# Scores of the first two head groups during the projection, x normalised on ScalarE, and a last tile in halves

## The chip, the cores and the metric

The kernel runs on one core of a Trainium2 chip. Its engines are TensorE (PE, matmul; loading weights is listed as PEld), VectorE (DVE), ScalarE (ACT), GpSimd (POOL), and SyncE (SP), which here issues every DMA. The metric is the device time of one execution in microseconds (us), lower is better. The kernel before took 815.09 us, the median of 3 runs (814.35 to 815.36).

## The reference

One block of cross attention and a feed-forward with ternary weights, each with a residual. All tensors are float32; batch 4, 512 rows each of x (512 wide) and of the context (256 wide), 32 heads of 16.

```python
q = rope((layernorm(x) @ Wq)), k = rope(ctx @ Wk), v = ctx @ Wv      # (4, 512, 32, 16) each
w = softmax(einsum('bqhd,bkhd->bhqk', q, k) / 4)
x = x + einsum('bhqk,bkhd->bqhd', w, v) @ Wout + bout
def bitlinear(x, w):
    xn = layer_norm(x)
    return absmax_quant(xn) @ ternarize_weights(w).T                 # 8-bit rows, weights in -g, 0, +g
h = gelu(bitlinear(layernorm(x), w_fc))                              # 512 -> 2048
x = x + bitlinear(h, w_proj)                                         # 2048 -> 512
```

## The kernel before

The program is written engine by engine. Each engine has a fixed list of instructions in the order of its block function, and semaphores join the lists. Nothing is scheduled by a planner: the order of the code is the order of the work.

**Projection.** The 2048 rows are 16 tiles of 128 rows. A loop `for s in range(3, TILES + 3)` runs on every engine with the tiles shifted against each other. A stage of TensorE turns the context of tile s-2 (`turn_ctx`, L256) and its normalised x (`turn_x`, L264), turns the rotated k of tile s-4 (`turn_rotated`, L304), multiplies tile s-3 by Wk and Wv (`project_kv`), turns the rotated q of s-4 and multiplies by Wq (`project_q`). Products are split: each operand has a rounded high part and a low part, and `product` (L279) runs high by high, high by low and low by high. Rotation (RoPE) is three products on VectorE (`rope_products`, L394 to L396) and a sum on GpSimd (`sum_products`, L486). The turned result is cut into three bfloat16 parts: cast on ScalarE (L459), subtraction on VectorE (`take_first`, L404), cast on ScalarE (L462), subtraction on GpSimd (`last_part`, L490). The layer norm of x takes statistics on VectorE (L375, L378), the root on GpSimd (`spread`, L477, L480) and the normalisation on VectorE (`normalise`, L384). SP loads inputs and pieces of the FFN weights, whose absolute values ScalarE sums, and after each second tile stores the parts to DRAM (`store_parts`). From there `load_stacks` brings them back, rearranged, as stacks of 96 rows for a group of 4 heads of one batch; it has 7 DMAs a group. There are 32 groups and 4 stack slots.

**Attention.** A step s does three things on TensorE (`tensor_step`): scores of group s with queries on the partitions (`scores`, L643, 16 matmuls in 8 pairs, two slots of two PSUM banks), of which VectorE takes row maxima (`row_maxima`, L713); scores of group s-2 turned round, with the maxima already subtracted by two more rows in the stack (`scores_turned`, L669), of which ScalarE takes exponentials (L733); and their product with v (`weigh_v`, L682). Between these, GpSimd splits the maxima (`split_maxima`), TensorE turns them, ScalarE saves them, and a small DMA (`load_max`, L575) puts them into the stack. GpSimd also makes a ternary weight block each step (`ternarise`, L762 to L767) and stages v. Scores of group 0 stand after the last q product, between the last turns; step 1 has scores of group 1 only. The ternary weights need the sum of all absolute values, so a totals matmul and a few small operations (`add_totals`, `weigh_ffn`) lie there too.

**Rows.** For 16 tiles again: output projection (`mix`, L901), quantisation, `expand` (L915), GELU, statistics of h (`statistics`, L982, L987), centring (`centre_h`, L1045), the largest value (L995) and clipping (L1004, L1010) in `clip_h`, the second float16 part (`second_h`, L1016), transposing DMAs of both parts (`turn_h`, L883), `contract` (L927, 32 matmuls a tile), and `finish` (L1023). For the last tile nothing stands beside this chain but the contraction of tile 14.

## Time and profile before

| | us |
|---|---|
| median of 3 runs | 815.09 |
| the profiled execution | 815.23 |
| its span (first to last instruction) | 813.3 |
| TensorE busy | 782.3 |
| VectorE busy | 679.5 |
| ScalarE busy | 452.3 |
| GpSimd busy | 332.6 |
| mean granted clock of TensorE | 0.979 of 2.4 GHz |

The profile describes one execution. Times of its rows are microseconds from the start of the span. "Idle before" is how long the engine stood still before an instruction, and the arrow names what ended the wait. A granted clock of 1.00 is 2.4 GHz, 0.50 is 1.2 GHz. The instructions of a line are pipelined, so the listed durations of matmuls overlap; what one costs the engine is read from the distance of starts or from the chain.

### The profile page before, as it was taken

Reading aid. Unit: us, or ns where it says so; the run is one execution under the profiler, and the core shown is the slowest. Engines: PE = TensorE matmul, PEld = TensorE weight load, DVE = VectorE, ACT = ScalarE, POOL = GpSimd, SP = SyncE. Lnnn points to the kernel's source line nnn. Section 1 sums busy time; section 2 is a strip of 40 time slices with the busy share of each in tenths; the row PEclk is TensorE's granted clock in tenths of the full one; section 3 lists DMA queues with packets and bytes.
Section 4 is the critical chain, followed back from the end, with each engine's and each line's share of the span. In section 5 each row is a group of like instructions: output and inputs, shape, how many; then the busy total and the mean of one; then the engine's idle time right before and its main releaser. Section 6 shows DMA issues by size and latency. Waiting matters only on the chain.

```text
span 813.3 us, 11712 instructions
## 1 busy us (share of the span) xinstructions
PE 782.3 (96%) x3844; PEld 333.6 (41%) x3844; DVE 679.5 (84%) x940; ACT 452.3 (56%) x828; POOL 332.6 (41%) x428
## 2 busy tenths in 40 slices
PE   3999997999999999999999999899999999999996
PEld 3788884122222222222322232244444444444442
DVE  6888887888888888888888888269999998988983
ACT  5567664277777777777777777734223432233330
POOL 2687776724543554455445544323212211111000
PEclk9999998599999999999999999999999999999999
DMA  7588887545465554667656653325556546553463
GB/s 260 156 221 261 236 227 183 122 110 127 125 170 138 153 145 133 154 142 164 163 155 166 172 167 80 84 64 122 109 123 151 111 90 117 109 125 79 78 130 90
DMA packets 173677, 116.17 MB, mean 143 GB/s; under 512 B 114562, under 2 KB 145330, under 8 KB 173618
## 3 DMA queue, kind: packets, MB, share of 16 engines
q1 hardware_dynamic: 173618, 115.44, 57.0%
q8 instruction: 31, 0.51, 0.3%
q14 instruction: 28, 0.23, 0.1%
HBM read 64.50 MB, written 25.43 MB: 111 GB/s over the span
## 4 chain that ended last, share of the span: by engine, by line
PE 86%; DVE 7%; DMA 2%; ACT 2%; issue 2%; POOL 2%; SPq 0%; DVEq 0%; POOLq 0%; ACTq 0%
PE banks L682 15%; PE banks L669 15%; PE banks L643 13%; PE banks L915 11%; PE banks L279 11%; PE banks L927 10%; PE banks L901 7%; PE banks L304 2%; DVE h_scales L995 1%; DMA stack_words<-max_rows 1%; DVE maxima L713 1%; DVE h_stats L982 1%; ACT probs_words L733 1%; PE banks L264 1%; ACT probs_words L1045 1%
## 5 line engine op out<-in xcount | busy, mean ns | idle before, releaser
L713 DVE TENSOR_REDUCE maxima<-banks 128x2 f32<-128x1024 f32 x256 | 302.0, 1216 | 52.1 <-PE banks L643 52.0
L733 ACT ACTIVATE probs_words<-banks 128x512 f32<-128x512 f32 x512 | 276.0, 597 | 101.3 <-PE banks L669 99.4
L669 PE MATMUL banks<-stack_words 98*128 98x512 bf16 x512 | 175.6, 386 | 2.7 <-ACT probs_words L733 1.8
L643 PE MATMUL banks<-stack_words 96*128 96x512 bf16 x512 | 160.2, 395 | 4.5 <-DVE maxima L713 3.9
L682 PE MATMUL banks<-probs_words,late_words 128*32 128x512 f32 x1024 | 137.2, 608 | 0.5
L927 PE MATMUL banks<-ternary_words,stack_words 128*128 128x512 f16 x512 | 114.6, 383 | 4.5 <-DMA stack_words<-stack_words 4.5
L915 PE MATMUL banks<-ternary_words,late_words 128*128 128x512 f16 x512 | 113.1, 379 | 0.0
L1045 ACT ACTIVATE probs_words<-probs_words,h_moments 128x2048 f32<-128x2048 f32 x16 | 32.0, 2002 | 135.8 <-DVE h_moments L987 135.8
L669 PEld LDWEIGHTS banks<-stack_words 98*128 98x128 bf16 x512 | 39.5, 97 | 144.2 <-ACT probs_words L733 84.3
L747 POOL TENSOR_SCALAR neg_max<-maxima 128x16 f32<-128x16 f32 x32 | 8.3, 258 | 175.0 <-DVE maxima L713 175.0
L927 PEld LDWEIGHTS banks<-ternary_words,stack_words 128*128 128x128 f16 x512 | 50.5, 99 | 70.0 <-issue 13.5
L643 PEld LDWEIGHTS banks<-stack_words 96*128 96x128 bf16 x512 | 49.7, 99 | 69.2 <-DVE maxima L713 13.4
L915 PEld LDWEIGHTS banks<-ternary_words,late_words 128*128 128x128 f16 x512 | 50.1, 98 | 61.4 <-issue 1.7
L1068 POOL TENSOR_SCALAR h_powers<-h_moments 128x1 f32<-128x1 f32 x16 | 3.6, 224 | 155.0 <-DVE h_moments L987 155.0
L1039 ACT ACTIVATE probs_words<-banks,row_scale 128x512 f32<-128x512 f32 x64 | 42.5, 683 | 29.1 <-PE banks L915 29.0
L901 PE MATMUL banks<-v_words,attn_words 128*128 128x512 f32 x128 | 57.6, 593 | 0.0
L762 POOL TENSOR_SCALAR late_words<-late_words,limits 128x512 f16<-128x512 f32 x32 | 50.2, 1568 | 0.0
L764 POOL TENSOR_SCALAR late_words<-late_words,limits 128x512 f16<-128x512 f32 x32 | 50.1, 1565 | 0.0
L490 POOL TENSOR_TENSOR ternary_words<-attn_words,ternary_words 128x512 bf16<-128x512 f32 x32 | 37.3, 1167 | 23.0 <-ACT ternary_words L462 23.0
L682 PEld LDWEIGHTS banks<-probs_words,late_words 128*32 128x32 f32 x1024 | 20.2, 108 | 54.6 <-ACT probs_words L733 39.8
L486 POOL TENSOR_TENSOR attn_words<-attn_words 128x512 f32<-128x512 f32 x32 | 41.3, 1291 | 2.0 <-DVE attn_words L396 0.9
L995 DVE TENSOR_REDUCE h_scales<-probs_words 128x1 f32<-128x2048 f32 x16 | 36.4, 2272 | 4.3 <-ACT probs_words L1045 4.3
(129 smaller groups left out, 932.1 us busy)
## 6 DMA issues: line engine op xcount, KB each, us to landing
o_rows<-late_words SPq DMA_DIRECT2D x32, 256.0 KB, 2.8
k_parts<-ternary_words SPq DMA_DIRECT2D x48, 128.0 KB, 3.2
q_parts<-ternary_words SPq DMA_DIRECT2D x48, 128.0 KB, 2.5
stack_words<-q_parts SPq DMA_DIRECT2D x32, 192.0 KB, 3.0
stack_words<-k_parts SPq DMA_DIRECT2D x96, 64.0 KB, 2.7
stack_words<-k_parts SPq DMA_DIRECT2D x32, 192.0 KB, 2.8
attn_words<-in_x_dram SPq DMA_DIRECT2D x16, 256.0 KB, 4.2
probs_words<-in_L_ffn_w_fc_dram SPq DMA_DIRECT2D x16, 256.0 KB, 3.3
```

What stands on the lines that cost most here:

```text
L279: mm = self.nc.tensor.matmul(out, lhs[a][:, slot, k * P:(k + 1) * P], rhs[b][:, k, :], start=(a + b + k == 0), stop=(a == 1 and k == count ...
L643: mm = self.nc.tensor.matmul(self.score_slot[j % 2][:, i], self.mem.q_stack[0:STACK, slot, head, c * P:(c + 1) * P], self.mem.k_stack[0:ST ...
L669: self.nc.tensor.matmul(self.mem.banks[:, self.ST_BANK[k]], self.mem.k_stack[0:STACK + 2, slot, head, c * P:(c + 1) * P], self.mem.q_stack ...
L682: mm = self.nc.tensor.matmul(self.pv_bank[32 * j:32 * j + 32], self.v_ones[:, g % 2, c, j, :], self.probs[:, c, j, :], start=(c == 0), sto ...
L713: dve.tensor_reduce(self.maxima[:, g % 2, 2 * j:2 * j + 2], self.score_slot[j % 2], AX.X, ALU.max).then_inc(self.scores_read, 1)
L733: act.activation(self.probs[:, c, head, :], self.mem.banks[:, self.ST_BANK[k]], ACT.Exp, scale=1 / math.sqrt(HEAD)).then_inc(self.exp_done, 1)
L762: pool.tensor_scalar(self.below[:], self.raw[:, w], limits[:, 1, w:w + 1], None, ALU.is_lt).then_inc(self.cut, 1)
L764: pool.tensor_scalar(self.ternary[:, w], self.raw[:, w], limits[:, 0, w:w + 1], None, ALU.is_gt).then_inc(self.cut, 1)
L901: mm = self.nc.tensor.matmul(self.y_bank[n % 2], att.attnT[:, n // CHUNKS * KX + k, c * P:(c + 1) * P], self.wout_sb[:, k, :], start=(k == ...
L915: mm = self.nc.tensor.matmul(self.fc_bank[o], self.uT[:, n % U_SLOTS, part * KX + k], self.fcT[:, k, o], start=(k + part == 0), stop=(k == ...
L927: mm = self.nc.tensor.matmul(self.proj_bank[r], self.hT[:, r, part, k], self.projT[:, k // 2, k % 2], start=(k + part == 0), stop=(part == ...
L995: dve.tensor_reduce(scale(0), now, AX.X, ALU.max, apply_absolute_value=True).then_inc(self.h_step, 1)
```

## The change

- Scores of groups 0 and 1 are taken as 32 single matmuls (`early_scores`), each into PSUM bank 7, each read by a reduction over 512 values (`early_maxima`) before the next may write. In the stages s = 10 to 18 of the projection there are three a stage; five more stand among the last turns and after them. The stacks of the groups 0 to 3 are loaded in the stages 8, 10, 13 and 15. The maxima of group 0 are split, turned, saved and loaded at the end of the projection. The attention loops begin with step 2.
- `normalise` moves from VectorE to ScalarE, between the two casts of k (`first_two` becomes `first_part` and `second_part`); GpSimd gets a third small instruction in `spread` for its bias.
- At the start `project_kv` is cut in two, so that the k product stands ahead of turning x; GpSimd takes the high parts of Wq for k = 1 and 3.
- ScalarE no longer waits for the stored parts; SP does, before its attention loop. GpSimd splits the maxima of group 1 and stages v before the first ternarisation.
- The last tile is centred, reduced, clipped, split and turned in two halves of 1024 columns, and its statistics come ahead of `second_h` of tile 14.

```diff
+    def normalise(self, act, n):
+        r = n % 2
+        act.wait_ge(self.rstd_ready, n + 1)
+        need(act, self.x_turned, n - 1)
+        act.activation(self.xn[:, r], self.x_sb[:, n % INPUT_SLOTS], ACT.Identity, bias=self.rstd[:, r, 2:3],
+                       scale=self.rstd[:, r, 1:2]).then_inc(self.xn_ready, 1)
...
+    def weight_high_too(self, pool, loaded, high, raw, ready):
+        pool.wait_ge(loaded, DMA)
+        pool.tensor_copy(high, raw).then_inc(ready, 1)
...
                            ).then_inc(self.power_ready, 1)
         pool.wait_ge(self.power_ready, n + 1)
         pool.tensor_tensor(self.rstd[:, r, 1:2], self.rstd[:, r, 0:1], self.mem.half_power[:], ALU.pow
+                           ).then_inc(self.power_taken, 1)
+        pool.wait_ge(self.power_taken, n + 1)
+        pool.tensor_scalar(self.rstd[:, r, 2:3], self.moments[:, r, 0:1], self.rstd[:, r, 1:2], -1.0, ALU.mult, ALU.mult
                            ).then_inc(self.rstd_ready, 1)
...
+    def early_scores(self, pe, i):
+
+        g, head, c = i // (GH * CHUNKS), i // CHUNKS % GH, i % CHUNKS
+        if i % (GH * CHUNKS) == 0:
+            pe.wait_ge(self.stacks_loaded[g], STACK_LOADS)
+        need(pe, self.early_read, i)
+        self.nc.tensor.matmul(self.early_bank, self.mem.q_stack[0:STACK, g, head, c * P:(c + 1) * P],
+                              self.mem.k_stack[0:STACK, g, head, :], start=True, stop=True).then_inc(self.early_ready, 1)
+
+    def turn_first_max(self, pe):
+        pe.wait_ge(self.split_ready, 1)
+        self.nc.tensor.transpose(self.early_max_bank, self.max_parts[:, 0], self.mem.identb[:]).then_inc(self.max_turned, 1)
...
-        if g == 0 and k == self.ST_BANK.index(self.TURN_BANK):
-            pe.wait_ge(self.max_saved, 1)
-        elif k != self.after_turn:
+        if g == 0 and k < 3:
+            pe.wait_ge(self.prj.multiplied[1], TILES)
+            for side in range(2):
+                pe.wait_ge(self.prj.rest_done[side], TILES)
...
+    def early_maxima(self, dve, i):
+        g, at = i // (GH * CHUNKS), i % (GH * CHUNKS)
+        dve.wait_ge(self.early_ready, i + 1)
+        dve.tensor_reduce(self.maxima[:, g, at:at + 1], self.early_bank, AX.X, ALU.max).then_inc(self.early_read, 1)
...
-        pool.wait_ge(self.scores_read, (g + 1) * 2 * GH)
+        if g < self.EARLY:
+            pool.wait_ge(self.early_read, (g + 1) * GH * CHUNKS)
+        else:
+            pool.wait_ge(self.scores_read, (g + 1 - self.EARLY) * 2 * GH)
...
+    def turn_last(self, sp, part, half):
+        n, k = TILES - 1, FFN // P // 2
+        r, done = n % 2, self.h_first if part == 0 else self.parts_ready
+        sp.wait_ge(done, n + 1 + half)
+        if part + half == 0:
+            need(sp, self.proj_ready, n - 1)
+        sp.dma_start_transpose(self.hT[:, r, part, half * k:(half + 1) * k], self.h_parts[:, r, part, half * HALF:(half + 1) * HALF]
+                               ).then_inc(self.last_turned[part][half], DMA)
...
+        for half in range(2):
+            dve.wait_ge(self.h_centred, n + 1 + half)
+            dve.tensor_reduce(self.half_max[:, half:half + 1], halves[half], AX.X, ALU.max, apply_absolute_value=True
+                              ).then_inc(self.halves_read, 1)
+        dve.wait_ge(self.halves_read, 2)
...
+        for half in range(2):
+            dve.tensor_scalar(halves[half], halves[half], scale(2), Q_B, ALU.mult, ALU.min).then_inc(self.last_clipped, 1)
+            dve.wait_ge(self.last_clipped, 1 + half)
+            dve.tensor_scalar(self.h_parts[:, r, 0, half * HALF:(half + 1) * HALF], halves[half], -Q_B, None, ALU.max
+                              ).then_inc(self.h_first, 1)
...
+            part = self.h_parts[:, r, :, half * HALF:(half + 1) * HALF]
+            dve.wait_ge(self.h_first, n + 1 + half)
+            dve.scalar_tensor_tensor(part[:, 1], halves[half], -Q_B, part[:, 0], ALU.max, ALU.subtract
+                                     ).then_inc(self.parts_ready, 1)
...
-                if s in (14, 16):
-                    att.load_stacks(sp, s // 2 - 7)
-            att.load_stacks(sp, 2)
-            att.load_stacks(sp, 3)
+                if s in (8, 10, 13, 15):
+                    att.load_stacks(sp, (8, 10, 13, 15).index(s))
+                if s == TILES + 3:
+                    att.load_max(sp, 0)
+            for pair in range(2):
+                sp.wait_ge(prj.parts_stored[pair], PAIR_STORES * BATCH)
...
-                    prj.project_kv(pe, s - 3)
+                    prj.project_k(pe, s - 3)
+                if s == TILES + 2:
+                    att.turn_first_max(pe)
+                if s >= 10:
+                    att.early_scores(pe, 3 * (s - 10))
+                if 1 <= s - 3 < TILES:
+                    prj.project_v(pe, s - 3)
                 if within(s - 4, TILES):
                     prj.turn_rotated(pe, s - 4, 1)
+                if s >= 10:
+                    att.early_scores(pe, 3 * (s - 10) + 1)
                 if within(s - 3, TILES):
                     prj.project_q(pe, s - 3)
-            att.scores(pe, 0, 0)
+                if s >= 10:
+                    att.early_scores(pe, 3 * (s - 10) + 2)
             prj.turn_rotated(pe, TILES - 1, 0)
-            att.scores(pe, 0, 1)
+            att.early_scores(pe, 27)
             prj.turn_rotated(pe, TILES - 1, 1)
-            att.scores(pe, 0, 2)
...
+            for i in range(28, att.SINGLES):
+                att.early_scores(pe, i)
+            pe.wait_ge(att.early_read, att.SINGLES)
             prj.add_totals(pe)
-            for j in range(3, 2 * GH):
-                att.scores(pe, 0, j)
-
-            for s in range(1, GROUPS + 3):
+
+            for s in range(2, GROUPS + 3):
                 att.tensor_step(pe, s)
                 if s >= GROUPS:
...
+                if s > 10:
+                    att.early_maxima(dve, 3 * (s - 11) + 2)
...
-                if within(s - 1, TILES):
-                    prj.normalise(dve, s - 1)
+                if s >= 10:
+                    att.early_maxima(dve, 3 * (s - 10))
                 if s < TILES:
...
+            prj.rope_products(dve, TILES - 1, 1)
+            att.early_maxima(dve, 26)
+            prj.take_first(dve, TILES - 1, 0)
+            att.early_maxima(dve, 27)
             prj.sum_ffn(dve)
-            prj.rope_products(dve, TILES - 1, 1)
-            att.row_maxima(dve, 0, 0)
-            prj.take_first(dve, TILES - 1, 0)
-            att.row_maxima(dve, 0, 1)
+            att.early_maxima(dve, 28)
             prj.take_first(dve, TILES - 1, 1)
-            att.row_maxima(dve, 0, 2)
+            for i in range(29, att.SINGLES):
+                att.early_maxima(dve, i)
             prj.weigh_ffn(dve)
-            for j in range(3, 2 * GH):
...
+                if s == TILES:
+                    rows.clip_last(dve)
+                    rows.finish(dve, s - 3)
+                    rows.split_last(dve)
...
-                    prj.first_two(act, s - 4, 0)
+                    prj.first_part(act, s - 4, 0)
+                if within(s - 1, TILES):
+                    prj.normalise(act, s - 1)
+                if within(s - 4, TILES):
...
-            for pair in range(2):
-                act.wait_ge(prj.parts_stored[pair], PAIR_STORES * BATCH)
...
+            att.split_maxima(pool, 1)
+            pool.wait_ge(prj.projected[1], TILES)
             pool.memset(att.v_ones, 1.0).then_inc(att.pads_ready, 1)
             pool.wait_ge(att.pads_ready, 1)
+            pool.wait_ge(prj.v_saved, TILES)
+            att.stage_v(pool, 0)
             for s in range(GROUPS + 1):
-                if s >= 1:
```

The order on TensorE in one stage of the projection, from the last part of the k product on (wk, wv and wq are the weights, ident is the matrix that turns a tile, stack_words holds the stacks). Before:

```order
L279 MATMUL banks<-wk_high,ctxT_low 128x512 x2
L279 MATMUL banks<-wv_high,ctxT_high 128x512 x2
L279 MATMUL banks<-wv_low,ctxT_high 128x512 x2
L279 MATMUL banks<-wv_high,ctxT_low 128x512 x2
L304 MATMUL banks<-ident,attn_words 128x128 x4
L279 MATMUL banks<-wq_high,xT_high 128x512 x4
L279 MATMUL banks<-wq_low,xT_high 128x512 x4
L279 MATMUL banks<-wq_high,xT_low 128x512 x4
L256 MATMUL banks<-ident,attn_words 128x128 x2
```

and now:

```order
L282 MATMUL banks<-wk_high,ctxT_low 128x512 x2
L679 MATMUL banks<-stack_words 128x512
L282 MATMUL banks<-wv_high,ctxT_high 128x512 x2
L282 MATMUL banks<-wv_low,ctxT_high 128x512 x2
L282 MATMUL banks<-wv_high,ctxT_low 128x512 x2
L311 MATMUL banks<-ident,attn_words 128x128 x4
L679 MATMUL banks<-stack_words 128x512
L282 MATMUL banks<-wq_high,xT_high 128x512 x4
L282 MATMUL banks<-wq_low,xT_high 128x512 x4
L282 MATMUL banks<-wq_high,xT_low 128x512 x4
L679 MATMUL banks<-stack_words 128x512
L259 MATMUL banks<-ident,attn_words 128x128 x2
```

Three score matmuls (L679) have come in, one before the v product, one before the q product, and one after it.

The order on VectorE around the same place, with the RoPE products (the first three rows, PSUM banks in, attn_words out), then the low parts and the subtraction. Before:

```order
L394 TENSOR_TENSOR attn_words<-banks,ternary_words 128x512
L395 TENSOR_TENSOR attn_words<-banks,ternary_words 128x64x4
L396 TENSOR_TENSOR attn_words<-banks,ternary_words 128x64x4
L416 TENSOR_TENSOR ctxT_low<-banks,ctxT_high 128x256
L423 TENSOR_TENSOR xT_low<-banks,xT_high 128x512
L404 TENSOR_TENSOR attn_words<-banks,ternary_words 128x512
L384 TENSOR_SCALAR ternary_words<-attn_words,project_moments,rstd 128x512
L375 BN_STATS project_stats<-attn_words 128x6
L378 BN_AGGR project_moments<-project_stats 128x2
L394 TENSOR_TENSOR attn_words<-banks,ternary_words 128x512
L395 TENSOR_TENSOR attn_words<-banks,ternary_words 128x64x4
L396 TENSOR_TENSOR attn_words<-banks,ternary_words 128x64x4
```

and now:

```order
L395 TENSOR_TENSOR attn_words<-banks,ternary_words 128x512
L396 TENSOR_TENSOR attn_words<-banks,ternary_words 128x64x4
L397 TENSOR_TENSOR attn_words<-banks,ternary_words 128x64x4
L753 TENSOR_REDUCE maxima<-banks 128x1
L417 TENSOR_TENSOR ctxT_low<-banks,ctxT_high 128x256
L424 TENSOR_TENSOR xT_low<-banks,xT_high 128x512
L405 TENSOR_TENSOR attn_words<-banks,ternary_words 128x512
L753 TENSOR_REDUCE maxima<-banks 128x1
L382 BN_STATS project_stats<-attn_words 128x6
L386 BN_AGGR project_moments<-project_stats 128x2
L395 TENSOR_TENSOR attn_words<-banks,ternary_words 128x512
L396 TENSOR_TENSOR attn_words<-banks,ternary_words 128x64x4
```

The normalisation (L384) is gone from the stage, and three reductions (L753) have come, one of them ahead of the low parts of context and x.

The order on TensorE at the end of the projection, from the last third of the last q product on (L311 and L318 now are the turns and the totals). Before:

```order
L279 MATMUL banks<-wq_high,xT_low 128x512 x4
L643 MATMUL banks<-stack_words 128x512 x2
L304 MATMUL banks<-ident,attn_words 128x128 x4
L643 MATMUL banks<-stack_words 128x512 x2
L304 MATMUL banks<-ident,attn_words 128x128 x4
L643 MATMUL banks<-stack_words 128x512 x2
L311 MATMUL banks<-abs_sum,ones 128x2
L643 MATMUL banks<-stack_words 128x512 x18
L652 MATMUL banks<-identb,max_parts 32x128
L643 MATMUL banks<-stack_words 128x512 x8
L669 MATMUL banks<-stack_words 128x512
```

and now:

```order
L282 MATMUL banks<-wq_high,xT_low 128x512 x4
L679 MATMUL banks<-stack_words 128x512
L311 MATMUL banks<-ident,attn_words 128x128 x4
L679 MATMUL banks<-stack_words 128x512
L311 MATMUL banks<-ident,attn_words 128x128 x4
L679 MATMUL banks<-stack_words 128x512 x4
L318 MATMUL banks<-abs_sum,ones 128x2
L709 MATMUL banks<-stack_words 128x512
L668 MATMUL banks<-stack_words 128x512 x2
L709 MATMUL banks<-stack_words 128x512 x3
L668 MATMUL banks<-stack_words 128x512 x2
```

32 score matmuls (L643, those of groups 0 and 1) stood between the last q product and the first turned scores (L669). Now six single ones (L679) and the totals stand there, and then step 2 begins (L709, L668).

The order on VectorE for the last tile (h_scales are its scales, probs_words is h, stack_words its parts). Before:

```order
L1006 SCALAR_TENSOR_TENSOR out_scale<-h_scales,gamma 128x1
L1010 TENSOR_SCALAR stack_words<-probs_words 128x2048
L1016 SCALAR_TENSOR_TENSOR stack_words<-probs_words,stack_words 128x2048
L982 BN_STATS h_stats<-probs_words 128x6 x4
L987 BN_AGGR h_moments<-h_stats 128x2
L1023 SCALAR_TENSOR_TENSOR v_words<-banks,out_scale,late_words 128x512
L995 TENSOR_REDUCE h_scales<-probs_words 128x1
L997 RECIPROCAL h_scales<-h_scales 128x1
L999 TENSOR_SCALAR h_scales<-h_scales 128x1
L1001 SCALAR_TENSOR_TENSOR h_scales<-h_scales,h_powers 128x1
L1004 TENSOR_SCALAR probs_words<-probs_words,h_scales 128x2048
L1006 SCALAR_TENSOR_TENSOR out_scale<-h_scales,gamma 128x1
```

and now:

```order
L1047 BN_STATS h_stats<-probs_words 128x6 x4
L1052 BN_AGGR h_moments<-h_stats 128x2
L1081 SCALAR_TENSOR_TENSOR stack_words<-probs_words,stack_words 128x2048
L1095 TENSOR_REDUCE v_words<-probs_words 128x1 x2
L1098 TENSOR_TENSOR h_scales<-v_words 128x1
L1100 RECIPROCAL h_scales<-h_scales 128x1
L1102 TENSOR_SCALAR h_scales<-h_scales 128x1
L1106 TENSOR_SCALAR probs_words<-probs_words,h_scales 128x1024
L1108 TENSOR_SCALAR stack_words<-probs_words 128x1024
L1106 TENSOR_SCALAR probs_words<-probs_words,h_scales 128x1024
L1108 TENSOR_SCALAR stack_words<-probs_words 128x1024
L1133 SCALAR_TENSOR_TENSOR v_words<-banks,out_scale,late_words 128x512
```

The statistics of tile 15 have moved ahead of the second part of tile 14 (L1081), and the reduction and the clipping are done in halves.

## Rows read from the trace of the kernel before

**Rows 1.** Page part 1, busy time and share of the span by engine.

```profile
PE 782.3 (96%) x3844; PEld 333.6 (41%) x3844; DVE 679.5 (84%) x940; ACT 452.3 (56%) x828; POOL 332.6 (41%) x428
```

**Rows 2.** Windows: us, busy (xinstructions) by engine, granted clock, DMA share; one stage.

```profile
75.79:82.85 7.06, 7.06 (x39) 5.93 (x38) 6.06 (x13) 4.88 (x12) 5.63 (x6) 1.00 0.89 278
```

**Rows 3.** Timeline, TensorE, turning ctx: start, us, engine, line, what.

```profile
82.85 0.38 PE L256 MATMUL banks<-ident,attn_words 128*128 128x128 f32 x2
...
89.92 0.38 PE L256 MATMUL banks<-ident,attn_words 128*128 128x128 f32 x2
```

**Rows 4.** Windows of 10 us at the end of the projection.

```profile
130.00:140.00 10.00, 6.42 (x28) 3.15 (x27) 8.76 (x15) 3.17 (x6) 6.17 (x6) 0.80 0.69 176
...
150.00:160.00 10.00, 9.06 (x23) 2.27 (x26) 8.29 (x8) 4.10 (x7) 9.69 (x11) 0.50 0.33 81
```

**Rows 5.** Chain of waits in order of time, 126 to 172: start, us, what.

```profile
131.82 0.45 PE banks L643 x2
...
151.63 2.68 DMA stack_words<-max_rows
...
154.44 0.59 PE banks L669
...
169.34 0.22 PE banks L669
```

**Rows 6.** Page part 5, costliest groups: busy us, mean ns, idle before.

```profile
L713 DVE TENSOR_REDUCE maxima<-banks 128x2 f32<-128x1024 f32 x256 | 302.0, 1216 | 52.1 <-PE banks L643 52.0
```

**Rows 7.** Chain of waits in order of time, 760 to the end.

```profile
786.36 2.48 DVE h_stats L982 x4
...
796.61 4.47 DMA stack_words<-stack_words
...
801.21 8.77 PE banks L927 x32
```

**Rows 8.** Windows of 2 us in the last contraction.

```profile
802.00:804.00 2.00, 2.00 (x6) 0.76 (x5) 0.00 (x0) 0.00 (x0) 0.00 (x0) 0.50 1.09 329
```

**Rows 9.** Timeline, TensorE, contraction of tiles 13 and 14.

```profile
782.77 13.98 PE L927 MATMUL banks<-ternary_words,stack_words 128*128 128x512 f16 x64
```

**Rows 10.** Timeline of the start, GpSimd and TensorE.

```profile
8.10 2.16 POOL L480 TENSOR_TENSOR rstd<-rstd,half_power 128x1 f32<-128x1 f32 x1
...
19.66 0.90 PE L264 MATMUL banks<-ident,ternary_words 128*128 128x128 f32 x4 [2.53 <-DVE ternary_words L384]
...
25.61 2.51 POOL L486 TENSOR_TENSOR attn_words<-attn_words 128x512 f32<-128x512 f32 x2
...
26.93 0.66 PE L304 MATMUL banks<-ident,attn_words 128*128 128x128 f32 x4 [1.62 <-POOL attn_words L486]
```

**Rows 11.** Groups by line, 60 to 130: busy us, mean ns | idle before.

```profile
L490 POOL TENSOR_TENSOR ternary_words<-attn_words,ternary_words 128x512 bf16<-128x512 f32 x20 | 23.4, 1168 | 13.3 <-ACT ternary_words L462 13.3
L404 DVE TENSOR_TENSOR attn_words<-banks,ternary_words 128x512 f32<-128x512 f32 x20 | 13.7, 686 | 6.5 <-issue 6.5
...
L462 ACT CAST ternary_words<-attn_words 128x512 bf16<-128x512 f32 x20 | 12.4, 619 | 20.0 <-DVE attn_words L404 20.0
...
L480 POOL TENSOR_TENSOR rstd<-rstd,half_power 128x1 f32<-128x1 f32 x8 | 4.5, 567 | 0.7
L384 DVE TENSOR_SCALAR ternary_words<-attn_words,project_moments,rstd 128x512 f32<-128x512 f32 x8 | 4.3, 538 | 0.0
```

**Rows 12.** Timeline of SP: load of x, loads of one group's stacks.

```profile
60.33 0.45 SPq L205 DMA_DIRECT2D attn_words<-in_x_dram  x1
...
101.23 1.45 SPq L570 DMA_DIRECT2D stack_words<-q_parts  x3
102.73 1.81 SPq L570 DMA_DIRECT2D stack_words<-k_parts  x4
```

**Rows 13.** DMA issues from 740 on: count, median us to landing.

```profile
stack_words<-stack_words SPq DMA_TRANSPOSE x10, 4.4
late_words<-late_words SPq DMA_TRANSPOSE x2, 3.1
```

184 lines of the change are left out of this document (124 added, 60 removed).

## The prediction

> **What bounds the kernel now.** I read the busy shares first. The reader is to see there that TensorE is busy nearly all of the span [rows 1]. So time can be saved only where it waits, works at its lower clock, or does work that could go; VectorE (DVE), with the second-largest share, is the one to follow next.
>
> Next the tables by stretch. In the projection (16 tiles, about 26 to 132 us) one stage of 7.06 us holds 7.06 us of TensorE, 6.06 of VectorE, 4.88 of ScalarE and 5.63 of GpSimd [rows 2]. The same instruction of two neighbouring stages starts 7.07 us apart [rows 3]. TensorE sets the pace there, and VectorE has 1.0 us to spare in each stage.
>
> Between 130 and 155 us TensorE works little and falls from 2.4 to 1.2 GHz: granted clock 0.80 in 130 to 140, 0.50 in 150 to 160 [rows 4]. The chain of waits tells why [rows 5]: after the last projection at 131.82 come row maxima of groups 0 and 1, sixteen reductions on VectorE of 1.22 us each [rows 6], and the hand-over of the maxima (POOL, DMA). The first turned scores run at 154.44, and the second attention step begins at 169.34, so that the step before it takes 14.9 us.
>
> At the end the chain leaves TensorE again [rows 7]: statistics of the last tile from 786.36, centring, reduction and clipping, a transposing DMA from 796.61 that lands 4.47 us later, then 32 matmuls in 8.77 us instead of 6.9, because the clock was granted at 0.50 in 802 to 804 [rows 8]. The 64 matmuls of tiles 13 and 14 took 13.98 us [rows 9].
>
> The profiled execution took 815.23 us: 813.3 of span and 1.9 around it. That is 0.14 above the median of the three runs (815.09), so I may work from it.
>
> **Term 1, the start: -1.7 us (0 to -2.5).** Now the k product of tile 0 stands ahead of turning its x, ScalarE normalises, GpSimd makes two of four high parts of Wq, and ScalarE's list is shorter. Today x of tile 1 is turned at 19.66, and GpSimd's first two RoPE sums run at 25.61, so TensorE can turn rotated k only at 26.93 [rows 10]. Walking the new lists: ScalarE has normalised tile 1 at about 17.3 (v of tile 0 is out at 15.0, then a copy, a cast and the normalisation, some 0.6 each). VectorE ends the four low parts of Wq at 20.0 instead of 21.5, since it no longer normalises between them. The statistics of tile 3 follow at 21.8, GpSimd's reciprocal root (one small instruction longer, 0.3) ends at 23.8, and its first sum at 25.1 instead of 26.9. If the GpSimd copies come late, nothing is left.
>
> GpSimd's power of 0.57 us [rows 11] took 2.16 at 8.10 [rows 10], while VectorE subtracted two SBUF tensors. The Trainium skill ("SBUF — State Buffer", section on the two separate sides) says that VectorE with two SBUF inputs and GpSimd hold one port pair as an exclusive lock. The trace agrees (2.16 against 0.57). By that rule the two new copies on GpSimd and the subtractions for Wq would block each other; that is rival B.
>
> **Term 2, the projection: +5.8 us (+5.5 to +8).** 26 of the 32 early score matmuls now stand before the end of the last q product, three a stage in stages 10 to 18 but for the last of them. One costs TensorE what it costs now: a pair at 131.82 took 0.45 us at full clock [rows 5], 0.22 each. 26 x 0.22 = 5.7, and the transposed maxima of group 0 add 0.1. Nothing hides this, since TensorE has no gap there. A stage becomes 7.07 + 0.66 = 7.73 us.
>
> Is VectorE still under it? It loses the normalisation, 0.54 us [rows 11], and gains three reductions over 512 values. No row shows a single one from PSUM. Below, it is half the double one, 0.61; above, the whole 1.22 [rows 6]; I take 0.66, as half of it and a small fixed part, since the 512-wide subtractions from PSUM last 0.69 [rows 11]. So 6.06 - 0.54 + 3 x 0.66 = 7.50 us, 0.2 under TensorE. At 1.22 each it would be 9.2 and 9 stages would cost 13 us more; the neighbours of the same width speak against that. The other loop: turn rotated k, cast, subtract, cast, then on GpSimd the third part (1.17), the root (now about 1.2) and the sum (1.26, half of the two at 25.61) [rows 10, 11], until rotated k is turned again. With the reduction that now stands ahead of the subtraction I get 7.5 us for it, also 0.2 under 7.73. ScalarE has 4.88 + 0.6 of work [rows 2], and the normalisation falls into its wait of 1.0 us between the two casts [rows 11], so it costs nothing; without that wait it would still fit into 7.73.
>
> The queue of SP: seven issues for a group's stacks take 1.45 + 1.81 = 3.3 us [rows 12], now in stages 8, 10, 13 and 15. The first also waits until the parts of tile 3 have landed, about 2.5 us. The load of x of tile 10 goes from 60.33 [rows 12] to about 66, lands by 70, and is wanted at 71.7 (stage 10 opens two periods before 82.85, three us into it). The cover is 1.7 us; later loads have 4 or more.
>
> **Term 3, the junction: -13.9 us (-11.5 to -15).** Count from the end of the last q product, 131.8 today. VectorE multiplies for 1.3 us, GpSimd sums for 1.26, rotated q is turned at 2.8 after it, as today. Behind it stand four single scores that share one PSUM bank with the one before, so matmul, reduction and two signals follow each other, 1.15 to 1.35 us a time, and the subtraction for q lies between the first and the second. The last is read at about 8.4; the totals matmul and the first turned scores follow at 8.7, as 140.5 on today's clock against 154.44 [rows 5]. The maxima of group 0 were loaded long before, so that chain is off the path. What is late next: v staged on GpSimd (142.1, wanted at 145.7) and the maxima of group 1. These go out only behind a weight load that waits for the second ternarisation, which ends at about 150.8; with the 2.7 us of today's transfer [rows 5] they land at 154.3, while the step of 14.9 us ends at 155.4. So I keep today's length for that step, at its low clock, and the second step begins at 155.4 instead of 169.34: 13.9 saved. If all single scores cost 1.6 us, 1.5 is lost; if the first step ran 1 us shorter, 1 is won and no more, because of the transfer.
>
> The attention steps after it and the row stage up to tile 14 keep their instructions and their TensorE pace: 0.
>
> **Term 4, the end: -5.7 us (-4.5 to -5.9).** The statistics of tile 15 now come before the second part of tile 14 (2.3 us), so they begin at 784.1, not 786.36 [rows 7]. Centring in two halves lets the reduction of the first half run beside that of the second. VectorE: second part of 14 until 789.1, two reductions over 1024 until 791.4 (1.18 apart), three scalars until 792.1, the halves clipped and stored as first part at 793.6 and 795.15, the residual of 13 (0.75), the second parts at 797.1 and 798.3. A transposing DMA over 2048 columns lands in 4.4 us, one over 1024 in 3.1 [rows 13]. The four halves therefore land at 796.8, 798.3, 800.3 and 801.5. TensorE needs them from 797.2 on, in steps of 1.73 us, so it never waits: 797.2, 798.9, 800.6, 802.4, end at 804.15. The second part of tile 14 is now later, issued at 789.1 and landed at 793.6, and TensorE wants it at 793.2; that 0.4 is in these numbers. Today the end is 809.98. Saved 5.8; I take 5.7. With 4.4 us for a half DMA the last half lands at 802.7, and 5.3 are saved; with a drop of the clock for half of the 32 matmuls, 4.5 or less.
>
> **The sum.** 815.23 - 1.7 + 5.8 - 13.9 - 5.7 = 799.7; on the median of the runs 799.6. I say 799.8.
>
> **Rivals.**
> A. VectorE or the k loop through GpSimd sets the stage. Both have only 0.2 us of room, and VectorE already waits 0.3 us a stage for signals at its subtraction (6.5 us before 20 of them [rows 11]). At 8.2 us a stage the nine stages cost 9 x 0.47 = 4.2 more: 804.0. For it: 97% filling of an in-order engine. Against: its inputs are all there early.
> B. The start brings nothing, as GpSimd's copies and VectorE's subtractions hold each other up: 1.7 more, 801.5. For it the 2.16 us of [rows 10]; against it, the copies have VectorE's PSUM work beside them.
> C. The change doesn't do what it says in part: scores wait at stage 10 for stacks, or the maxima of group 1 land late after the junction. The first is a single stall of up to 3 us, the second moves the second step to 157; 802.5.
> D. The other side: SP's queue becomes the bound. A pair of stages holds about 11.3 us of issues today and 14.6 with a set of stacks, against 15.5 for two stages. If waits inside the stores did not shrink and a pair took 24 us, three pairs, less a prefetch of about 8 us, would cost 17 us: 817. It decides against the change from 23 us a pair on. Against it: the x loads of today are issued 8 to 12 us early.
>
> **How the numbers follow.** Forecast 0.60; A 0.20 (804.0); B 0.10 (801.5); C 0.07 (802.5); D 0.03 (817). The range must hold A and the better ends of terms 1 and 3 (1 + 1 us) and a little of term 2: 796.5 to 805.5, which leaves out D and bad ends of A. What a measurement here tells from no change is about 0.2%, 1.6 us. Faster by more than that 0.96, within it 0.01, slower 0.03.
>
> **What would show it.** In the profile after: start of the repeated projection stage 1.7 us earlier; distance of stages 10 to 18 of 7.7 us with VectorE at about 97% and no gap on TensorE; last q product ending at about 136; first turned scores 8.7 us after it; second step 23.6 after it; no idle time of TensorE over 0.5 us in the last 20 us and a granted clock of 1.00 there. I am wrong if a stage takes over 8 us (A), if single reductions take over 0.75 us, if TensorE waits at the first early score, or if the half transposes land 4 us or more after issue.

## The result and the profile after

The changed kernel takes 801.72 us (median of 4 runs, 800.98 to 801.96), the kernel before 814.72 beside it: ratio 0.9837, 95% interval 0.9822 to 0.9852, so 13.0 us faster. One execution of run 10 below (821.30 us, granted clock 0.947, where its other four have 0.989 to 0.994) is set aside, and as it was the profiled one, no trace of run 10 is used. The changed kernel's profiled execution took 800.98 us, the shortest of its four, with a span of 799.1. The busy line of the page [rows 1]:

```profile
PE 773.6 (97%) x3844; PEld 332.4 (42%) x3844; DVE 674.0 (84%) x945; ACT 462.0 (58%) x843; POOL 340.2 (43%) x446
```

TensorE has the same 3844 matmuls and 8.7 us less of them by time; fewer run at the low clock, as the windows below show. A landmark is an event that both traces have. I cut both at the same five:

| term | landmark | before | after | difference | predicted |
|---|---|---|---|---|---|
| 1 start | first turn of rotated k | 26.93 | 25.75 | -1.2 | -1.7 |
| 2 projection | end of last q product | 131.83 | 137.03 | +6.4 | +5.8 |
| 3 junction | sixth block of weighted v | 176.08 | 167.22 | -14.1 | -13.9 |
| attention, rows | contraction of tile 13 starts | 782.77 | 774.21 | +0.3 | 0 |
| 4 end | last matmul ends | 809.98 | 795.84 | -5.6 | -5.7 |
| sum | | | | -14.2 | -15.5 |

Each difference is the change of the distance to the landmark above it. The sixth block of weighted v is the sixth group of eight `weigh_v` matmuls, in the second attention step. The sum of -14.2 is that of two profiled executions, and more than the 13.0 of the medians. The projection in windows, two stages [rows 2]:

```profile
75.27:83.00 7.73, 7.73 (x42) 6.17 (x41) 7.29 (x16) 5.37 (x12) 5.68 (x7) 1.00 0.88 230
83.00:90.77 7.77, 7.77 (x43) 6.18 (x42) 7.32 (x16) 5.63 (x13) 5.90 (x8) 1.00 1.01 305
```

and TensorE turning ctx in the timeline [rows 3]:

```profile
75.27 0.39 PE L259 MATMUL banks<-ident,attn_words 128*128 128x128 f32 x2
...
83.00 0.38 PE L259 MATMUL banks<-ident,attn_words 128*128 128x128 f32 x2
...
90.77 0.38 PE L259 MATMUL banks<-ident,attn_words 128*128 128x128 f32 x2
```

7.73 and 7.77 us a stage, all of it TensorE; VectorE is at 7.3. The windows behind it [rows 4]: the clock was half granted for one stretch of 10 us only (140.2 to 150.4).

```profile
130.00:140.00 10.00, 8.11 (x41) 5.81 (x40) 8.34 (x17) 5.11 (x12) 7.58 (x9) 1.00 0.54 142
140.00:150.00 10.00, 6.86 (x19) 2.41 (x19) 6.60 (x13) 4.93 (x8) 5.91 (x9) 0.51 0.69 161
150.00:160.00 10.00, 9.06 (x50) 2.44 (x47) 7.97 (x7) 6.72 (x13) 9.66 (x9) 0.98 0.41 74
```

The junction in the timeline (start, us, engine, line, out<-in, idle time before and what ended it) [rows 5]. L679 are single early scores, L753 their reductions, L318 the totals, L709 turned scores:

```profile
141.82 0.61 PE L679 MATMUL banks<-stack_words 96*128 96x512 bf16 x1 [0.79 <-DVE maxima L753]
...
142.47 0.69 DVE L753 TENSOR_REDUCE maxima<-banks 128x1 f32<-128x512 f32 x1
...
143.22 0.61 PE L679 MATMUL banks<-stack_words 96*128 96x512 bf16 x1 [0.79 <-DVE maxima L753]
...
146.00 0.59 PE L318 MATMUL banks<-abs_sum,ones 128*128 128x2 f32 x2 [0.79 <-DVE maxima L753]
...
146.45 0.59 PE L709 MATMUL banks<-stack_words 98*128 98x512 bf16 x1
...
157.33 0.40 SPq L608 DMA_DIRECT2D late_words<-in_L_ffn_w_proj_dram  x1
...
157.79 0.71 SPq L598 DMA_DIRECT2D stack_words<-max_rows  x1
...
160.31 0.39 PE L709 MATMUL banks<-stack_words 98*128 98x512 bf16 x1 [1.25 <-DVE maxima L759]
```

A single score and its reduction repeat every 1.40 us. The second step starts at 160.31 after 1.25 us of waiting; the profile names L759, which had ended before, but the load of the row maxima was issued at 157.79, behind the weight load (L608), so the DMA is what was late (run 7 puts that to the test).

The end in the timeline [rows 7, 9] (L1047 statistics, L1095 half maxima, L992 contraction):

```profile
774.21 10.52 PE L992 MATMUL banks<-ternary_words,stack_words 128*128 128x512 f16 x48
775.39 2.47 DVE L1047 BATCH_NORM_STATS2 h_stats<-probs_words 128x6 f32<-128x512 f32 x4
...
780.22 2.33 DVE L1095 TENSOR_REDUCE v_words<-probs_words 128x1 f32<-128x1024 f32 x2
...
785.29 10.53 PE L992 MATMUL banks<-ternary_words,stack_words 128*128 128x512 f16 x48 [0.56 <-DMA stack_words<-stack_words]
```

The wait of 0.56 us is for the transposed second part of tile 14; the prediction had 0.4 for it in its numbers and 0.5 as the limit for any idle time there. The clock is 1.00, where it was 0.50 [rows 8]:

```profile
790.00:795.00 5.00, 5.00 (x24) 2.25 (x23) 0.00 (x0) 0.00 (x0) 0.00 (x0) 1.00 0.63 171
```

### The profile page after: what moved, and what is told of

It is laid out like the page before. It is cut to its first block, busy times and chain, and to the rows that moved or that the text cites. A ratio compares the mean times of both kernels' runs of the same rounds, so it can differ in the third digit from the quotient of the medians.

```text
span 799.1 us, 11757 instructions
## 1 busy us (share of the span) xinstructions
PE 773.6 (97%) x3844; PEld 332.4 (42%) x3844; DVE 674.0 (84%) x945; ACT 462.0 (58%) x843; POOL 340.2 (43%) x446
## 4 chain that ended last, share of the span: by engine, by line
PE 87%; DVE 6%; ACT 2%; DMA 2%; issue 2%; POOL 1%; SPq 0%; DVEq 0%; POOLq 0%; ACTq 0%
PE banks L723 16%; PE banks L709 15%; PE banks L668 13%; PE banks L977 11%; PE banks L992 11%; PE banks L282 10%; PE banks L963 7%; PE banks L311 2%; PE banks L679 1%; DVE h_stats L1047 1%; ACT probs_words L779 1%; DVE h_scales L1060 1%; PE banks L267 1%; DMA stack_words<-max_rows 1%; DMA stack_words<-stack_words 1%
## 5 line engine op out<-in xcount | busy, mean ns | idle before, releaser
L759 DVE TENSOR_REDUCE maxima<-banks 128x2 f32<-128x1024 f32 x240 | 283.1, 1216 | 49.9 <-PE banks L668 49.9
L709 PE MATMUL banks<-stack_words 98*128 98x512 bf16 x512 | 175.0, 385 | 3.7 <-ACT probs_words L779 1.8
L668 PE MATMUL banks<-stack_words 96*128 96x512 bf16 x480 | 144.2, 381 | 0.0
L992 PE MATMUL banks<-ternary_words,stack_words 128*128 128x512 f16 x512 | 113.0, 379 | 0.6 <-DMA stack_words<-stack_words 0.6
L977 PE MATMUL banks<-ternary_words,late_words 128*128 128x512 f16 x512 | 113.1, 379 | 0.0
L1155 ACT ACTIVATE probs_words<-probs_words,h_moments 128x2048 f32<-128x2048 f32 (+1 forms) x17 | 32.2, 1901 | 134.4 <-DVE h_moments L1052 134.4
L709 PEld LDWEIGHTS banks<-stack_words 98*128 98x128 bf16 x512 | 39.6, 97 | 144.3 <-ACT probs_words L779 85.1
L992 PEld LDWEIGHTS banks<-ternary_words,stack_words 128*128 128x128 f16 x512 | 50.0, 98 | 64.9 <-issue 6.3
L1178 POOL TENSOR_SCALAR h_powers<-h_moments 128x1 f32<-128x1 f32 x16 | 5.5, 343 | 152.9 <-DVE h_moments L1052 152.9
L668 PEld LDWEIGHTS banks<-stack_words 96*128 96x128 bf16 x480 | 47.4, 99 | 53.4 <-issue 1.1
L507 POOL TENSOR_TENSOR ternary_words<-attn_words,ternary_words 128x512 bf16<-128x512 f32 x32 | 37.3, 1166 | 23.2 <-ACT ternary_words L472 22.4
L1047 DVE BATCH_NORM_STATS2 h_stats<-probs_words 128x6 f32<-128x512 f32 x64 | 39.4, 678 | 0.0
```

The source lines that it names most:

```text
L668: mm = self.nc.tensor.matmul(self.score_slot[j % 2][:, i], self.mem.q_stack[0:STACK, slot, head, c * P:(c + 1) * P], self.mem.k_stack[0:ST ...
L709: self.nc.tensor.matmul(self.mem.banks[:, self.ST_BANK[k]], self.mem.k_stack[0:STACK + 2, slot, head, c * P:(c + 1) * P], self.mem.q_stack ...
L759: dve.tensor_reduce(self.maxima[:, g % 2, 2 * j:2 * j + 2], self.score_slot[j % 2], AX.X, ALU.max).then_inc(self.scores_read, 1)
L977: mm = self.nc.tensor.matmul(self.fc_bank[o], self.uT[:, n % U_SLOTS, part * KX + k], self.fcT[:, k, o], start=(k + part == 0), stop=(k == ...
L992: mm = self.nc.tensor.matmul(self.proj_bank[r], self.hT[:, r, part, k], self.projT[:, k // 2, k % 2], start=(k + part == 0), stop=(part == ...
L1047: dve.bn_stats(self.h_stats[:, o], self.h[:, n % H_SLOTS, o * DIM:(o + 1) * DIM]).then_inc(self.h_stats_done, 1)
```

## Experiments

Each run is the changed kernel with one edit, or with several together in 9 and 12. Ratios are to the kernel before, run beside it; for the changed kernel it is 0.9837 (0.9822 to 0.9852). The intervals are 1 to 2 us to either side, so smaller effects are read from landmarks of one profiled execution. How far these repeat: from the end of the last q product to the sixth block of weighted v there are 29.9 to 30.3 us in the six profiled executions that have the junction unchanged (changed kernel, runs 2 to 5 and 11). The kernel before was profiled once.

**1. Early scores off.** The loops of all engines at the junction are as before (ScalarE waits for the stored parts again), but the stacks of the groups 0 to 3 are still loaded early. The edit, shortened:

```diff
-    EARLY = 2
+    EARLY = 0
...
-                if s >= 10:
-                    att.early_scores(pe, 3 * (s - 10))   # and the other early calls
...
+            att.scores(pe, 0, 0)   # ... pairs behind the projection
```

> No early scores: groups 0 and 1 are scored in pairs after the projection as in the kernel before, group 0 turned in step 2 of the loop. Start, normalisation on ScalarE, order of k, v and q, early stacks and tail as in the changed kernel. My theory (junction term -14.1 and projection term +6.4 both belong to the early scores alone; the normalisation's move only makes room on VectorE): the projection stage returns to 7.07 us, the first turned scores of the second step come 22 to 23 us after the last q product; 801.7 + 14.1 - 5.8 = 810.0 us, 808.0 to 811.0. Rival 1 (part of the stage's growth comes from the new ScalarE order, so the stage stays near 7.3): 811 to 812.5. Rival 2 (the early stack loads and the other order at the junction bring much of the gain by themselves): 803 to 807.

807.61 us, ratio 0.9911 (0.9887 to 0.9935). TensorE turns x every 7.06 us again (84.11, 91.18, 98.24), so the 0.7 us a stage are the scores' alone. From the end of the last q product (132.86) to the sixth block of weighted v are 42.0 us, against 44.3 before and 30.2 after. So 11.8 of the 14.1 us belong to the early scores; 2.3 remain without them. Where, the clock tells. Kernel before, then this one:

```profile
136.00:138.00 2.00, 1.03 (x2) 0.13 (x2) 1.91 (x4) 0.70 (x2) 1.24 (x2) 0.50 0.49 114
...
162.00:164.00 2.00, 2.00 (x8) 0.58 (x7) 0.55 (x1) 1.41 (x4) 0.00 (x0) 0.68 0.00 0
```

```profile
138.00:140.00 2.00, 0.91 (x2) 0.11 (x2) 1.97 (x3) 0.55 (x1) 1.37 (x2) 0.81 0.87 196
...
158.00:160.00 2.00, 2.00 (x7) 0.61 (x4) 1.10 (x1) 1.37 (x3) 2.00 (x3) 0.57 0.39 130
```

The first turned scores come as late as before (22.4 us after the q product, 22.6 before), but the half clock lasts about 20 us instead of 27, and the step behind them is shorter. I had expected 810.0. The two halves of the bargain (a longer projection, a shorter junction) belong together as claimed, and my price for losing it was 2.4 too high, about these 2.3. What shortens the low stretch is not shown: the stacks are loaded early in this run, but TensorE's waits are nearly the same in the two traces, and each is one execution.

**2. One reduction in three doubled.**

```diff
         dve.wait_ge(self.early_ready, i + 1)
+        if i % 3 == 1 and i < 24:
+            dve.tensor_reduce(self.neg_max[:, 1, at:at + 1], self.early_bank, AX.X, ALU.max)
```

> One of the three early reductions of each stage 10 to 17 is issued twice (its first result goes to an unused place): 0.68 us more VectorE per stage, nothing else. My theory (TensorE with 7.76 us bounds the stage, VectorE has 0.45 us of room): VectorE 7.98 us becomes the bound, stage about 8.0 us, 8 stages x 0.25 = +2 us: 803.7, 803.0 to 805.0. Rival 1 (VectorE is already the bound through its waits): the full 8 x 0.68 = 5.4 us, 807.1. Rival 2 (there is room in the order): 801.7, unchanged.

801.61 us, 0.9834 (0.9807 to 0.9861): nothing. Rival 2 held. VectorE in this run, window and timeline:

```profile
83.00:90.77 7.77, 7.77 (x43) 6.19 (x42) 7.74 (x17) 4.59 (x12) 5.80 (x8) 1.00 0.88 272
```

```profile
97.27 0.67 DVE L395 TENSOR_TENSOR attn_words<-banks,ternary_words 128x512 f32<-128x512 f32 x1
97.86 0.41 DVE L396 TENSOR_TENSOR attn_words<-banks,ternary_words 128x256 f32<-128x256 f32 x1
98.19 0.41 DVE L397 TENSOR_TENSOR attn_words<-banks,ternary_words 128x256 f32<-128x256 f32 x1
98.52 0.68 DVE L754 TENSOR_REDUCE neg_max<-banks 128x1 f32<-128x512 f32 x1
99.12 0.68 DVE L755 TENSOR_REDUCE maxima<-banks 128x1 f32<-128x512 f32 x1
```

Records of 0.68 us start 0.60 apart: neighbours overlap by 0.08. The extra reduction went where VectorE had stood idle (it waited 0.42 us a stage for TensorE): VectorE's busy time in this window rose from 7.32 to 7.74 us of 7.77. The stages went from 7.74 to 7.76 us to 7.73 to 7.84, 0.2 us in all, the 7.84 in two of them. VectorE can run at 99% here, so rival A (at 97% a stage takes 8.2 us) has no footing.

**3. Normalisation back on VectorE, from tile 2 on.**

```diff
-                    prj.normalise(act, s - 1)
+                    prj.normalise_dve(dve, s - 1)   # behind take_first(s - 4, 0)
```

> From tile 2 on x is normalised by VectorE again, at its place of the kernel before (behind the subtraction of k's part); tiles 0 and 1, the early scores, and all other orders as in the changed kernel. VectorE's records start 0.60 us apart for a reduction recorded with 0.68, and 0.45 for the normalisation recorded with 0.54, and VectorE stands 0.42 us idle in a stage of 7.76. My theory (the move made the room that the early scores took, but just so): VectorE at the brim, stage 7.76 to 7.85 in the eight stages with early scores, +0 to +0.8 us: 802.1, 801.5 to 803.0. Rival 1 (x(n) is now normalised too late for TensorE, since it stands behind more of VectorE's work): stage 8.2 and more, 805 to 808. Rival 2 (the move to ScalarE itself cost something): 801 or less.

803.24 us, 0.9852 (0.9838 to 0.9865). TensorE turns x at 85.88, 93.63, 101.39, 109.17 and 117.01: 7.75 to 7.84 us a stage, and a window shows VectorE at the brim:

```profile
91.00:99.00 8.00, 8.00 (x44) 6.34 (x43) 7.96 (x17) 4.95 (x12) 6.06 (x8) 1.00 0.90 250
```

That is 0.1 us in all (63.32 to 124.79 against 60.69 to 122.03 in the changed kernel). The median lies 1.5 us up, inside my range, but the stages don't show why, and the intervals overlap. In the profile the tile turned at 63.32 is already 2.6 us late; what differs lies ahead of the early scores, in the start (see below). Moving the normalisation was hardly needed for the early scores.

**4. Tail undone; 5. only the order of the statistics kept.**

```diff
-                if s == TILES:
-                    rows.clip_last(dve)      # and split_last, turn_last, halves in centre_h
...
-                if s == TILES - 1:           # this one back in run 5
-                    rows.statistics(dve, s)
```

> The last tile's rows as in the kernel before: whole-tile centring, maximum, clipping and splitting, two whole transposes for part and remainder, its statistics again behind second_h of tile 14. All else as in the changed kernel. My theory (the tail term -5.6 us is independent of everything ahead of it): 801.7 + 5.6 = 807.3 us, 806.8 to 807.8. Rival (most of what the profiles show at the end is the clock, which a different run could grant at the old order too): 801.7 to 804. In the profile the contraction of tile 15 starts with the granted clock at 0.50 again.

> As the run with the whole tail undone, but the statistics of tile 15 stay ahead of second_h of tile 14; no halves. My theory: the last tile's chain is shortened by the one second_h that stood in front of its statistics, 2.2 us, so 801.7 + 3.4 = 805.1 us, 804.3 to 805.8, and the halves are worth the other 3.4. Rival 1 (order is all of it): 801.7. Rival 2 (moving second_h of tile 14 back delays the contraction of tile 14 by as much, and the chain ends with that): 807.3, no gain over the undone tail.

Undone: 806.84 us, 0.9904 (0.9878 to 0.9930). Order alone: 806.25, 0.9894 (0.9867 to 0.9920). From the start of tile 13's contraction to the end of the last residual are 27.9, 27.3 and 22.4 us (undone, order alone, changed). So the tail is worth 5.5, as predicted, but the order alone 0.6 and not 2.2; its 806.25 lies outside the 804.3 to 805.8 that I gave. In both runs the clock is half granted for 3.4 us at the last contraction (794.9 to 798.3 in run 4). With the order alone:

```profile
778.77 2.23 DVE L1079 SCALAR_TENSOR_TENSOR stack_words<-probs_words,stack_words 128x2048 f16<-128x2048 f32 x1
...
782.01 0.75 DVE L1131 SCALAR_TENSOR_TENSOR v_words<-banks,out_scale,late_words 128x512 f32<-128x512 f32 x1 [1.02 <-PE banks L990]
782.68 2.28 DVE L1058 TENSOR_REDUCE h_scales<-probs_words 128x1 f32<-128x2048 f32 x1
...
792.63 8.75 PE L990 MATMUL banks<-ternary_words,stack_words 128*128 128x512 f16 x32 [3.17 <-DMA stack_words<-stack_words]
```

The residual of tile 13 (782.01) stands ahead of the reduction and waits 1.02 us for TensorE, so earlier statistics gain little; the changed kernel moves this residual behind the clipping. TensorE still idles 3.2 us before the last 32 matmuls, and these take 8.75 us again.

**6. Four banks for the last four early scores.**

```diff
-        self.early_bank = banks[:, 7]
+        self.early_bank = lambda i: banks[:, 7 if i < self.SINGLES - CHUNKS else i % CHUNKS]
...
-        need(pe, self.early_read, i)
+        if i < self.SINGLES - CHUNKS:
+            need(pe, self.early_read, i)
...
```

> The last four early scores (the second head half of group 1's last head) go into four banks of their own (0 to 3, free by then) instead of the one shared bank 7, so that TensorE issues them without waiting for VectorE in between; step 2 waits for their reductions bank pair by bank pair. My theory (behind the last rotated q a round of product, signal, reduction, signal costs 1.4 us at the half clock, a reduction alone 0.68): three rounds save 0.7 us each, and the first turned scores no longer wait for the last of them: -2 to -3.5 us, 799.0 us (798.2 to 800.0). Rival 1 (the second step's wait for the row maxima of group 1 sets the end, and their DMA is issued late behind the weight load whatever happens here): 801.2 to 802. Rival 2 (VectorE is late with the last tile's subtraction): 800.5.

800.12 us, 0.9823 (0.9810 to 0.9837). The timeline:

```profile
142.55 1.91 PE L681 MATMUL banks<-stack_words 96*128 96x512 bf16 x4
...
144.43 1.88 DVE L755 TENSOR_REDUCE maxima<-banks 128x1 f32<-128x512 f32 x3
...
144.66 0.59 PE L711 MATMUL banks<-stack_words 98*128 98x512 bf16 x1
...
158.00 0.71 SPq L598 DMA_DIRECT2D stack_words<-max_rows  x1
...
160.12 0.39 PE L711 MATMUL banks<-stack_words 98*128 98x512 bf16 x1 [0.93 <-DMA stack_words<-max_rows]
```

The first turned scores come 5.6 us after the q product instead of 9.4, but the sixth block only 2.2 earlier. The clock takes the difference back: the step lasts 15.5 us instead of 13.9, as the low clock (142.4 to 152.6) covers 8 us of it instead of 4. The wait for the late load of the maxima is still there, 0.93 us at 160.12. My theory and rival 1 were each half right, and the time lies just above my 798.2 to 800.0.

**7. Row maxima of group 1 first; 8. the same in every step.** SP's loop, run 7 (run 8: in each step):

```diff
+                if s == 3:
+                    att.load_max(sp, s - 2)
                 if 2 <= s < GROUPS:
                     att.load_weight(sp, w_fc, w_proj, s)
...
-                if 1 <= s - 2 < GROUPS:
+                if 2 <= s - 2 < GROUPS:
                     att.load_max(sp, s - 2)
```

> On the DMA queue's engine the row maxima of group 1 are loaded ahead of weight 3, stacks 3 and the sums in step 3; the other steps as in the changed kernel. My theory (TensorE stood 1.25 us at 159.06 because the load of the row maxima was issued behind weight 3, which waited for the second ternarisation): up to -1.2 us, 800.7 us (800.4 to 801.2). Rival (weight 3 and its ternarisation come late instead, or the ExpS of ScalarE set the step): 801.7, unchanged.

> The same in every step: the row maxima are loaded ahead of the next weight and the next stacks. My theory: the first step gives up to -1.2 us as with the one step alone; in the steady state a step is set by ScalarE's exponentials, with a DMA wait for the row maxima every so often in the chain (5.7 us at 317.75), so a further 0 to -2 us; 800.2 us (798.7 to 801.2). Rival (the stacks and weights are issued later than before, as they wait behind the maxima of a group that comes late in the step; the stack loads then hold up the scores): 802 to 812.

Once: 800.59 us (799.40 to 804.43), 0.9845 (0.9821 to 0.9869); the time can't tell it from no change, the landmark says -1.0 (29.2 us to the sixth block), and the wait before the second step is gone. In every step: 862.93 us, 1.0602 (1.0574 to 1.0629). The rival won, far beyond its range. Waits of TensorE from 170 to 440 us (us in total, times, longest), then SP and TensorE in one step:

```profile
PE banks L668 <- DMA stack_words<-k_parts: 34.0, 19, 2.8
```

```profile
405.75 0.70 SPq L598 DMA_DIRECT2D stack_words<-max_rows  x1
407.03 1.31 SPq L593 DMA_DIRECT2D stack_words<-q_parts  x3
...
408.38 2.03 SPq L593 DMA_DIRECT2D stack_words<-k_parts  x4
...
412.92 0.90 PE L668 MATMUL banks<-stack_words 96*128 96x512 bf16 x2 [1.64 <-DMA stack_words<-k_parts]
...
420.76 0.68 SPq L598 DMA_DIRECT2D stack_words<-max_rows  x1
```

The stacks of the next group go out behind maxima that exist only in the middle of the step, their scores start late, and so do the next maxima. A step takes 15.0 us here (420.76 - 405.75), against 11.2 in the changed kernel (mean of the three from 400.95 to 434.47). In those 270 us the changed kernel's TensorE waits 0.4 us for DMA in all, and its mean granted clock is 1.00 where this run has 0.96.

**9. Both, four banks and maxima first once.** Diffs as above.

> Four banks and the row maxima of group 1 first. My theory: the two add up, 801.7 - 2.7 - 1.2 = 797.8 us (797.0 to 799.3), since four banks bring the maxima of group 1 forward and the load order then no longer holds them back. Rival (four banks alone already reach the bound of the second ternarisation, and this adds nothing, or the other way round): 799 to 800.7.

798.69 us, 0.9811 (0.9793 to 0.9828). The sixth block comes 26.9 us after the q product, 3.3 earlier than in the changed kernel; alone the two gave 2.2 and 1.0. By the landmark they add up; the time is inside my range.

**10. Start undone; 11. no casts on GpSimd.** Run 10 has the old order of the start on all engines; run 11 only this:

```diff
-            for k in (0, 2):                 # ScalarE; 1 and 3 on GpSimd
+            for k in range(KX):              # ScalarE, none on GpSimd
```

> The start as in the kernel before: x 0 turned ahead of k, statistics 1 behind the first rotation products, tiles 0 and 1 normalised on VectorE, all four high parts of Wq on ScalarE, the sines ahead of the high part of Wv. From tile 2 on everything as in the changed kernel, early scores and tail included. The prediction put this part at -1.7 us; the changed kernel's profile has -1.2 at the first turned k, but with early scores switched off the projection ended 1.0 us later than in the kernel before, since the 3.4 us of half clock that follow TensorE's waits fell on 26.7 to 30 us, where the products stand close, and not on 17.7 to 21. Theory now: the start is worth between -1.2 and +1.0 depending on where this stretch falls: 801.0 to 803.0 us, best guess 801.9. The prediction's own: 803.4. Rival (the new order costs as such): 800.0 to 800.8.

> All four high parts of Wq are cast by ScalarE, in order, at the same place in its program; GpSimd has none of them. All else as in the changed kernel. If GpSimd's two casts (2.0 us for the two) are what VectorE waited for (0.65 us at 17.05) and nothing else: 0 to -0.6 us. If two more casts on ScalarE (0.6 us each) delay its context save and normalisation of tile 1 that stand behind them: +0.6 to +1.2 us, 802.3 to 802.9. Rival from the prediction (GpSimd's casts and VectorE's subtractions hold each other up at the SBUF port, and that is why the start did not gain): -1 us or more, 800.7 or less. My value: 802.3, 801.2 to 803.2; in the profile VectorE's four subtractions take less than 4.5 us if the port held them up.

Start undone: 802.63 us (median of four), 0.9844 (0.9827 to 0.9861). The times can't tell a start worth 1.2 from one worth nothing. No casts on GpSimd: 800.45 us, 0.9814 (0.9799 to 0.9828), 1.9 us less than the changed kernel by the ratios, with intervals that overlap. My 802.3 missed; the rival's 800.7 or less was met. Changed kernel (groups by line from 16.0 to 16.9), then this one (16.6 to 17.0):

```profile
L411 DVE TENSOR_TENSOR wq_low<-probs_words,wq_high 128x512 fp32r<-128x512 f32 x1 | 1.7, 1681 | 0.0
```

```profile
L411 DVE TENSOR_TENSOR wq_low<-probs_words,wq_high 128x512 fp32r<-128x512 f32 x1 | 1.0, 1012 | 0.0
```

Beside GpSimd's casts (14.91 to 16.95) the first subtraction took 1.68 us; without them, and in the other three of the changed kernel, 1.01 to 1.02. So rival B's mechanism is there, for 0.66 us once. It repeats: in nine of the ten profiled executions with casts the four subtractions take 4.4 to 4.6 us together. They take 3.9 in the tenth (run 4), where they start only after the casts, and 3.8 in both without casts (runs 11 and 12). The Trainium skill ("SBUF — State Buffer", on the two separate sides) says that a VectorE instruction with two SBUF inputs and a GpSimd instruction that reads SBUF shut each other out of one shared port pair; the trace agrees as far as the delay goes.

The first turn of rotated k stands at 25.64 against 25.75, so this run's gain isn't pinned there: x of tile 1 landed 0.7 us later in this execution (its statistics start at 12.53 against 11.84), and the two casts more on ScalarE put the turn of that x at 19.74 instead of 17.42.

**12. Three edits together** (runs 9 and 11).

> Three edits to the changed kernel: four banks for the last four early scores, the row maxima of group 1 loaded ahead of weight 3, and all four high parts of Wq cast by ScalarE. The first two together gave 798.7 us (0.9811 of the kernel before), the third alone 800.5 us (0.9814), the changed kernel 801.7 (0.9837). My theory (the third acts in the start, the first two at the junction, so they add up): 0.979 of the kernel before, 797.5 us, 796.5 to 798.7. Rival (the third alone only had the stretch of half clock in a kinder place, and adds nothing): 798.7.

797.57 us (795.82 to 798.19), 0.9772 (0.9752 to 0.9793): 4.2 us under the changed kernel by the medians, its interval clear of it, and the fastest of all. The junction gave 3.3 (26.9 us to the sixth block, as in run 9). The third edit adds 1.1 us to run 9 by the medians; the intervals of the two just touch, so that it adds anything is not shown by the times.

## Why the prediction was right

The time (801.7 against 799.8) is in the range, and 1.9 us above the forecast. The bargain was as predicted: the projection pays for the scores at TensorE's pace, and the junction gives more back. Run 1 shows both halves. (The sum on record gives 799.6 on the median; I said 799.8 without a reason for the rest.) But the range had been opened for rival A, which did not happen. What the profiles show above the forecast lies mostly in the start and in where the half clock falls there, which no rival named. The changed kernel's own profile flatters this: it is the shortest execution of its four, and it shows -14.2 where the medians have -13.0 and I had forecast -15.3.

Term 3, the largest, came out at -14.1 against -13.9, with two errors that cancelled; that it was so close is luck. The first turned scores came 9.4 us after the last q product, not 8.7: a round of single score and reduction takes 1.40 us at half clock, above my 1.15 to 1.35. And "I keep today's length for that step, at its low clock" failed in its reason: the step took 13.9 us and not 14.9, because the full clock came back about 4 us into it and not 9. By subtraction it would have been 12.6 but for the wait of 1.25 us for the maxima of group 1, which I had named as what is late next; in run 7, without the wait, it took 13.2. Run 6 took the rounds away.

Term 2 was 0.6 too small in this profile. The stage is 7.73 to 7.77 (I said 7.73), a single score 0.23, a reduction 0.68 (I said 0.66), and VectorE's 7.3 lies below my 7.50. Eight whole stages make 8 x 0.69 = 5.5, two more scores and the transposed maxima 0.6, a wait of TensorE for these maxima 0.17 (at 131.7), which I had not seen.

Term 1 was predicted as -1.7. The profile shows -1.2. The casts on GpSimd were priced at nothing and held up a subtraction for 0.66 us: VectorE ends the four low parts of Wq at 20.6 and not at 20.0, and GpSimd its first sum at 25.7 and not at 25.1. ScalarE's normalisation takes 0.81 and not 0.6, but ended at 17.4 against my 17.3. Nor does -1.2 repeat. In the eight other profiled executions with this start (runs 1, 2 and 4 to 9) the first rotated k is turned at 25.7 to 26.6, which is -1.2 to -0.3. With one exception (run 4) the late ones are those in which x of tile 1 lands late: VectorE waits for that load in all nine, and its statistics start at 11.7 to 11.8 in the three early ones and at 12.3 to 12.8 in the five late ones.

The clock comes on top. In run 1, with the same start, the projection ended 1.0 us later than in the kernel before, although its stages are as long: the half clock fell on dense products from 26.6 to 30.0 us. In the changed kernel's profile it fell on 17.3 to 20.7 (windows of half a microsecond), and TensorE has waits left behind it, for ScalarE and GpSimd, that can take up what it loses there:

```profile
16.00:18.00 2.00, 0.58 (x3) 0.58 (x4) 2.00 (x3) 1.37 (x3) 0.95 (x1) 0.83 0.81 292
18.00:20.00 2.00, 2.00 (x7) 1.66 (x6) 2.00 (x3) 0.59 (x1) 0.00 (x0) 0.50 0.85 240
```

```profile
23.65 0.66 PE L267 MATMUL banks<-ident,ternary_words 128*128 128x128 f32 x4 [1.05 <-ACT ternary_words L456]
25.75 0.66 PE L311 MATMUL banks<-ident,attn_words 128*128 128x128 f32 x4 [1.44 <-POOL attn_words L503]
```

```profile
28.00:30.00 2.00, 2.00 (x6) 1.59 (x5) 1.50 (x4) 1.88 (x5) 0.48 (x1) 0.50 0.00 0
```

(The last row is run 1's.) From the first turn of rotated k to the end of the last q product there are 111.3 us where no half clock falls behind that turn (changed kernel and runs 5, 11, 12), 112.8 to 113.1 with a stretch of 3.4 us behind it or across it (runs 2, 3, 4, 6, 8, 9), and 114.0 with one of 6.8 us across it (run 7). The kernels of runs 4 to 9 have the same code as the changed one up to the last q product, and it ended at 137.0 (changed kernel and run 5), 138.9 (run 4), 139.0 (run 9), 139.1 (run 6), 139.5 (run 8) and 140.3 (run 7). Against 131.8 in the one profile of the kernel before, terms 1 and 2 together are +5.2 in the most favourable of these and +7.2 in the middle one, where I had +4.1.

So the step that failed is term 1: I priced a list of instructions, with the casts at nothing and x of tile 1 always there in time, and left the clock out. What the runs show in its place is -0.3 to -1.2 us at the landmark, and behind it a clock that costs 0, 1.5 to 1.8 or 2.7 us. Whether the new start is worth anything on the median stays open, as the kernel before has but one profile. Without the casts the q product ended at 136.9 and 137.5 (runs 11 and 12); of the nine executions with casts and early scores only two are as early (137.0). TensorE comes to the first rotated k without a wait there, and the half clock lies ahead of it (17.2 to 24.0 and 18.2 to 25.0). Two executions do not show that this is the rule.

Term 4 held (-5.6 against -5.7), but "2.3 us" for the earlier statistics was a wrong share: alone they give 0.6; they pay only with the halves and the residual moved. The 6.9 us for 32 matmuls at full clock were 0.1 short, as [rows 9] already gives 13.98 for 64.

Rivals: A is refuted by run 2, where VectorE at 99% cost 0.2 us. (Its wait of 0.3 us a stage was misread: 6.5 us before 20 subtractions are 0.3 each, and there are two a stage.) B's mechanism is real and small. C's second half happened, for 1.25 us. D did not happen in the changed kernel: the first stacks went out at 60.7 us and no load of x came late in the stages. Run 8 shows that SP's order can indeed cost 61 us.

## What to carry over

Work can be moved into a stretch that TensorE bounds and be charged at its matmul time alone, 0.7 us a stage here, as long as the engine that reads the results has room; it pays if it removes a longer serial stretch later (11.8 us), and what the serial stretch costs includes the half clock behind it. When matmuls and reductions alternate over one bank, four banks for the last four bring what follows forward (3.8 us here, of which 2.2 were left in the next step). The order of an in-order DMA queue is changed only at the place where a wait was seen; the same edit in every step cost 61 us. And a landmark of one profile is not a median: the same code reached the same landmark 3.3 us apart.

## What the hardware showed unexpectedly

- Neighbouring VectorE records overlap: 0.68 us each, started 0.60 apart (512 values), 0.41 and 0.33 (256 values). Sums of durations overstate VectorE's load by a tenth or more.
- The half clock in the start appears in every profile read here, but its place moves: 17.2 to 24.0 us in run 11, 17.3 to 20.7 in the changed kernel, 19.9 to 23.4 in the kernel before, 25.3 to 32.1 in run 7, 26.6 to 30.0 in run 1, and twice in run 8 (17.1 to 20.6 and 27.4 to 30.8). The same code up to the last q product ended at 137.0 in one execution and at 140.3 in another.
- A VectorE subtraction of two SBUF tensors went from 1.01 to 1.68 us beside a GpSimd cast.
- How long the clock stays at half after the projection differs: 10 us in the changed kernel (140.2 to 150.4), 20 in run 1 (139.2 to 159.7), 27 in the kernel before (136.0 to 163.3), though TensorE's waits in the last two are nearly alike. What makes the difference between these two is open.
